# Swin block, linear attention and experts on one core: output projection, scores and values in side-by-side pieces of the array, gates spread by DMA, a 16-group body

## What is computed

```python
# layer 0: windows of 7x7, shifted by 3, 8 heads of 8 channels
y = _ln(x, ln1_w, ln1_b);  win = windows(roll(y, -3))          # 64 windows of 49 positions per image
attn = softmax(q @ k.T * 8**-0.5 + bias[rel_index] + attn_mask)
x = x + roll(windows_back((attn @ v) @ proj_w.T + proj_b), 3)
h = gelu(_ln(x, ln2_w, ln2_b) @ fc1_w.T + fc1_b)               # 256 hidden channels
x = x + _ln(h, ln3_w, ln3_b) @ fc2_w.T + fc2_b
# layer 1a: linear attention over a whole image, 16 heads of 4 channels, k and v normed per head
u = _ln_t(x);  kv = sum_n(k_n v_n.T) / 3136;  t = x + gelu((q @ kv + u) @ W_proj.T + b_proj) + u
# layer 1b: 8 experts per position, the 2 with the largest router logits
xn = _ln_t(t);  logits = xn @ Wr + br;  w, idx = top-2 softmax weights
e_i = gelu(norm(xn) * ln_g[i] + ln_b[i]) @ W1[i] + b1[i]) @ W2[i] + b2[i]
out = t + sum over the 2 chosen experts of w_i * e_i
```

## Time and profile before

| | before |
|---|---|
| median of 3 runs | 10356.69 us (10355.85 to 10370.08) |
| span of the profiled execution, first to last instruction | 10332.3 us |
| TensorE busy | 9863.4 us, 95% of the span |
| VectorE, ScalarE, GpSimd busy | 8358.3, 6196.1, 5266.7 us (81%, 60%, 51%) |
| mean granted TensorE clock | 0.978 |
| DMA | 6 GB/s |

### The profile page before, as it was taken

How to read it: one execution, slowest core, us unless ns; L and a number is a source line. 1 busy time by engine, 2 the same in 40 slices (tenths; PEclk the granted TensorE clock), 3 DMA queues, 4 the chain that set the end, 5 groups by cost and what they waited for, 6 DMA issues and landing times.

```text
span 10332.3 us, 296342 instructions
## 1 busy us (share of the span) xinstructions
PE 9863.4 (95%) x88046; PEld 8285.3 (80%) x88046; DVE 8358.3 (81%) x30953; ACT 6196.1 (60%) x10499; POOL 5266.7 (51%) x8196
## 2 busy tenths in 40 slices
PE   6799999999999999999999999999999999999998
PEld 4578888888888888888888888888888888888877
DVE  4478888888888888888888888888888888888873
ACT  1356666666666666666666666666666666666653
POOL 1245555555555555555555555555555555555542
PEclk9989999999999999999999999999999999999997
DMA  0000000000000000000000000000000000000000
GB/s 19 2 5 5 6 6 6 5 6 6 6 5 6 6 6 5 6 6 5 6 6 6 5 6 6 5 6 6 6 5 6 6 5 5 6 6 5 6 4 4
DMA packets 63043, 57.40 MB, mean 6 GB/s; under 512 B 11731, under 2 KB 62456, under 8 KB 62584
## 3 DMA queue, kind: packets, MB, share of 16 engines
q1 hardware_dynamic: 62840, 55.45, 1.8%
HBM read 29.57 MB, written 25.69 MB: 5 GB/s over the span
## 4 chain that ended last, share of the span: by engine, by line
PE 83%; DVE 11%; issue 4%; ACT 1%; POOL 1%; SPq 0%; DVEq 0%; DMA 0%; ACTq 0%; POOLq 0%
PE ps L704 22%; PE ps L695 12%; PE ps L512 7%; PE ps L488 7%; PE ps L440 5%; PE ps L551 4%; PE ps L576 3%; DVE hid L810 3%; PE ps L480 3%; PE ps L499 3%; PE ps L594 2%; DVE kvr L934 2%; PE ps L566 2%; PE ps L686 2%; PE ps L668 2%
## 5 line engine op out<-in xcount | busy, mean ns | idle before, releaser
L704 PEld LDWEIGHTS ps<-we,ht 128*98 128x98 f32 x32768 | 3149.3, 171 | 194.7 <-issue 90.3
L704 PE MATMUL ps<-we,ht 128*98 128x64 f32 x32768 | 3229.3, 253 | 39.2 <-DVE yg L1070 39.1
L1309 ACT ACTIVATE ht<-ps,be 128x392 f32<-128x392 f32 x4096 | 2283.7, 584 | 1279.9 <-PE ps L695 651.0
L1194 POOL TENSOR_TENSOR yacc<-yacc,yg 98x256 f32 (+1 forms) x1792 | 1385.1, 773 | 328.5 <-DVE yg L1070 265.6
L695 PE MATMUL ps<-xs,we_hi 128*128 128x392 f16 x4096 | 1386.1, 338 | 10.7 <-ACT ht L1309 10.3
L695 PE MATMUL ps<-xs,we_lo 128*128 128x392 f16 x4096 | 1378.0, 336 | 0.0
L1070 DVE TENSOR_TENSOR yg<-ps,gate 98x256 f32<-98x256 f32 x2048 | 860.8, 420 | 526.3 <-PE ps L704 473.3
L1125 POOL TENSOR_TENSOR sc<-sc,mx 98x392 f32<-98x392 f32 x1024 | 857.1, 847 | 528.7 <-DVE mx L854 524.9
L1135 POOL TENSOR_TENSOR x1b<-x,fc2bias 98x256 f32<-98x256 f32 x256 | 213.2, 833 | 1514.3 <-DVE x L888 1514.3
L488 PE MATMUL ps<-kexp,qbd 128*98 128x392 f32 x2048 | 895.8, 520 | 19.8 <-DVE sc L848 10.4
L233 POOL TENSOR_TENSOR kexp<-kt,cs 128x392 f32<-128x392 f32 x512 | 438.4, 856 | 855.0 <-ACT kt L1216 855.0
(11 more groups left out here) (175 smaller groups left out, 20077.8 us busy)
## 6 DMA issues: line engine op xcount, KB each, us to landing
xg<-in_x SPq DMA_DIRECT2D x256, 98.0 KB
out_y<-yo SPq DMA_DIRECT2D x256, 98.0 KB
bias<-in_rel SPq DMA_DIRECT2D x1, 1200.5 KB
bias<-in_w SPq DMA_DIRECT2D x2, 512.0 KB
tu_img<-in_amask SPq DMA_DIRECT2D x2, 300.1 KB
we<-in_w SPq DMA_DIRECT2D x1, 512.0 KB
cs<-in_cst SPq DMA_DIRECT2D x1, 163.0 KB
ht<-ht SPq DMA_DIRECT2D x2, 75.0 KB
```

What stands on the lines that cost most here:

```text
L704: last = pe.matmul(pY[0:TOK, C * t:C * (t + 1)], ht[:, 2 * (e % 2) + h, cols(t)], we2[:, 2 * e + h, :], start=(h == 0), stop=(h == 1))
L1194: pool.tensor_tensor(dst, acc, yg[:, e % 2:e % 2 + 1, :], ALU.add).then_inc(S["y_sum"], 1)
L1309: act.activation(ht[:, b % 4, :], pH[b % 2][:, 0:GTOK], ACT.Gelu, bias=be1[:, b:b + 1], scale=1.0 / WSCALE).then_inc(S["h_ready"], 1)
```

## The change

It rewrites most of the pipeline. Number of operations and shapes are for one group; the line numbers with L are those of the new file where they differ.

1. **Experts' output** (`expert_out`). The operands change places: `we2` (128x64) is the weight and the 392 positions of `ht` stream. Two experts stand side by side, one in the left 64 columns of the array and one in the right 64, and write different partitions of pY. Sixteen products of 392 columns take the place of 64 of 64 columns.
2. **Gates.** Since positions are now columns, a gate has to be spread over 64 partitions. The turned gates go to DRAM and come back with a copy per partition (`gates_away`, `gates_back`: one DMA of 12 KB out and four of 196 KB in). VectorE multiplies and adds the bias in one operation of 128x392 per pair of experts (`expert`), GpSimd adds three times, TensorE turns the sum back with a product against two stacked identities (`combine`), and `finish` on VectorE adds the residual. `gbias` and the eight small multiplications and additions go.
3. **Scores.** Eight products per pair of tiles, each with 32 rows and 64 columns of the array, 196 columns streaming: heads 0 to 3 and 4 to 7 in different rows and banks, the two windows in different columns. The zero blocks in `qbd` go (ScalarE copies the queries as they are), `kexp` has half the columns, and scores lie on 113 partitions (0 to 48 and 64 to 112).
4. **Values.** The values (98x32 for two heads) are the weight, 49 columns of the turned probabilities stream, four pieces side by side in the array. ScalarE copies the output, TensorE turns it back (four transposes of 128 columns, `back`), and VectorE needs one reciprocal and one multiplication.
5. **Third norm.** Its mean is subtracted in `wf2` beforehand, its scale is multiplied after `fc2` (`t`: four operations of 98x64). `ln3n` goes.
6. **Router.** xn is split into two f16 halves before it is turned over, logits come from f16 products with both halves. `max` and `max_index`, which give the eight largest values and their places, once a tile, take the place of the 13 steps.
7. **Buffers and body.** Ring buffers are addressed by constants in a body of 16 groups; statistics are kept twice; u and the residual stay in one buffer of 16 groups each; the second copy of the turned u and its copy back (`utk`, `utc`) go. The order of all steps is new: attention is now up to 4 groups ahead, experts 8 to 10 back.

```diff
-XBUF, YBUF = 4, 8
+BODY = 16
+XBUF, YBUF = 4, 2
...
             def score(a, t):
...
-                pe.matmul(pS[0:TOK, 0:HEADS * WA], qbd[:, t, :], kexp[:, t, :], start=True, stop=True)\
+                for t2 in range(2):
+                    t = 2 * pair + t2
+                    for half in range(2):
+                        for w in range(2):
+                            chans = slice(C * w + 32 * half, C * w + 32 * (half + 1))
+                            last = pe.matmul((pS, pO)[half][C * w:C * (w + 1), 4 * WA * t2:4 * WA * (t2 + 1)],
+                                             qs[chans, TOK * t + WA * w:TOK * t + WA * w + C], kexp[chans, t, :],
...
             def attend(a, t):
...
-                for h in range(HEADS // 2):
-                    last = pe.matmul(o[:, :, 2 * h:2 * h + 2, :], pt[:, t % 2, h, :],
-                                     vexp[:, 2 * t:2 * t + 2, 2 * h:2 * h + 2, :], start=True, stop=True)
+                for w in range(2):
+                    for hp in range(HEADS // 2):
+                        last = pe.matmul(pO[32 * hp:32 * (hp + 1), TOK * t + WA * w:TOK * t + WA * (w + 1)],
+                                         vexp[:, 2 * t + w, 2 * hp:2 * hp + 2, :].rearrange("p h d -> p (h d)"),
+                                         pt[:, t, hp, WA * w:WA * (w + 1)], start=True, stop=True)
...
+            def back(g):
+                bank_free(pe, "oT", g)
+                now(pe, "o_kept", g)
+                for t in range(GT):
+                    last = pe.transpose(pP[0:TOK, 128 * t:128 * (t + 1)], os_[:, cols(t)], ident)
...
-            def expert_out(d, e):
-                now(pe, "h_ready", d, 2 * e + 1)
-                now(pe, "yg_ready", d - (e == 0), (e - 1) % NE)
-                for t in range(GT):
-                    for h in range(2):
-                        last = pe.matmul(pY[0:TOK, C * t:C * (t + 1)], ht[:, 2 * (e % 2) + h, cols(t)], we2[:, 2 * e + h, :],
-                                         start=(h == 0), stop=(h == 1))
+            def expert_out(g, p):
+                bank_free(pe, f"out{p}", g)
+                now(pe, "h_ready", g, 0, 4 * p + 3)
+                for h in range(2):
+                    for e in range(2):
+                        b = 4 * p + 2 * e + h
+                        last = pe.matmul(pY[C * e:C * (e + 1), 0:GTOK], we2[:, b, :], ht[:, b % 8, :],
+                                         start=(h == 0), stop=(h == 1), skip_group_check=True)
+            def combine(g):
+                bank_free(pe, "comb", g)
+                now(pe, "y_sum", g)
+                for t in range(GT):
+                    last = pe.matmul(pY[0:TOK, C * t:C * (t + 1)], yg[:, 0, cols(t)], ii[:, :], start=True, stop=True)
...
+            def gates_back(g, half):
+                if half == 0:
+                    sp.wait_ge(gates_out, 16 * (g.n + 1))
+                now(sp, "yg_ready", g, -1, 2 * half + 1, alone="sp")
+                for e in range(2):
+                    sp.dma_start(gb[C * e:C * (e + 1), 2 * half:2 * half + 2, :],
+                                 gates_dram[g.j % 2].rearrange("(p e) q -> e p q", e=2)[e, 2 * half:2 * half + 2]
+                                 .partition_broadcast(C)).then_inc(gates_in[half], 16)
...
-            def ln3n(n, j):
-                normalize(n, "3", hn, lambda t: hid[:, t, :], "hn_ready")
+                for t in range(GT):
+                    last = dve.scalar_tensor_tensor(out=tt[:, g.j % 2, t, :], in0=pB[0:TOK, C * t:C * (t + 1)],
+                                                    scalar=rs["3"][:, g.j % 2, t:t + 1], in1=x1b[:, t, :],
+                                                    op0=ALU.mult, op1=ALU.add)
...
+                for t in range(GT):
+                    last = dve.max(best[:, t, :], lg[:, t, :])
+                for t in range(GT):
+                    dve.max_index(which[:, g.j % 2, t, :], best[:, t, :], lg[:, t, :])
```

More of the change, by code:

```diff
@@ L717, in _ @@
-            for b in range(2 * NE):
-                steps[f"in{b}"] = lambda d, j, b=b: expert_in(d, b)
-            for e in range(NE):
-                steps[f"out{e}"] = lambda d, j, e=e: expert_out(d, e)
-            for part in range(5):
-                steps[f"mix{part}"] = lambda i, j, part=part: mix(i, part)
-            images(pe, PLAN["pe"], steps)
+                steps[f"s{half}"] = lambda g, half=half: score(g, half)
+                steps[f"fc1{half}"] = lambda g, half=half: fc1(g, half)
@@ L726, in _ @@
+                steps[f"hT{half}"] = lambda g, half=half: hidden_T(g, half)
+            for b in range(BLOCKS):
+                steps[f"in{b}"] = lambda g, b=b: expert_in(g, b)
+            for p in range(PAIRS):
+                steps[f"out{p}"] = lambda g, p=p: expert_out(g, p)
+            for part in range(4):
+                steps[f"mixp{part}"] = lambda g, part=part: mix(g, part)
+            program(pe, PLAN["pe"], steps)
         @block.vector
-        def _(ve_):
-            dve = ve_
+        def _(dve):
+            dve.memset(gb[:, :, :], 0.0).then_inc(setup_dve, 1)
@@ L1316, in _ @@
+            steps = dict(zt=ln1n, qs=queries, kt=keys, os=keep_o, ot=oT, z2t=z2t, uts=keep_ut, sq=kv, sd=deviation, lpg=gp_,
+                         xh=split_high, xs=keep_xs, tanh=route, gtt=gates, exp=softmax_exp)
+            for half in range(2):
+                steps[f"ge{half}"] = lambda g, half=half: gelu(g, half)
+                steps[f"hnt{half}"] = lambda g, half=half: keep_hidden_T(g, half)
             for t in range(GT):
-                steps[f"pt{t}"] = lambda a, j, t=t: keep_pt(a, t)
```

1494 lines of the change are left out of this document (727 added, 767 removed).

## The result

| | before | after |
|---|---|---|
| median of 4 runs | 10362.67 us (10355.85 to 10370.08) | 8551.73 us (8542.04 to 8556.77) |
| ratio, 95% interval | | 0.8252 (0.8242 to 0.8262) |
| span of the profiled execution | 10332.3 us | 8551.3 us |
| mean granted TensorE clock | 0.978 | 0.984 |

The changed kernel takes 17.5% less time. The forecast of 8970 us had the sign and, within its range, the size, but lay 418 us too high; the number of rival (b), 8507 us, lay 45 us too low and was the nearer one.

What follows compares the result with a forecast made beforehand. TensorE was taken to bound the kernel: its terms sum to -5.7 us a group, 38.4 to 32.7, 32.8 with waits. 243 groups give 7970 us, plus 980 and 24: 8974, said as 8970; range 8450 to 9700.

Steps and rivals of the forecast that it cites:

- Experts' output: TensorE's expert products, two running side by side: 1.53 us a block, 6.1 us a group against 10.9, so -4.8.
- Scores: TensorE's score products, all four places at once: 0.9 us a block, 1.8 against 2.7 a group, -0.9, at worst +0.4.
- Values: TensorE's value products, four pieces at once: 0.45 + 0.25 us a block, 2.8 a group, +0.1, bounds -1.0 and +3.5.
- (b): Rival, everything as hoped: values at 0.2 us a block and waits gone, 31.0 us a group, 8507 us; 13%.
- allowance for waits: TensorE's own waits stay about the same; 0.1 us a group added, 32.7 to 32.8.
- Small steps: TensorE's other steps a group: logits -0.45 us, turned xn -0.1, turned probabilities +0.2, `back` +0.43, `combine` +0.69.
- The changes of form: Entering or leaving another form of TensorE's array costs 0.09 to 0.10 us each way, 22 times a group against six.
- all fit: The other engines' lists stay under 32.7 us a group: VectorE about 24, ScalarE 25.1, GpSimd about 18.
- Head and tail: Time outside the steady stretch, set-up included: left at 980 us of the 999 before.
- (a): Rival, waits between the lists from ScalarE, late gates or slower value records: 35.5 us a group, 9650 us; 22% with (d).
- (d): Rival, TensorE's clock falls to 1.2 GHz more often: some 2 us a group, near 9500 us; 22% with (a).
- (c): Rival, the array's pieces run one after another: +4.7 us, 43.1 us a group, 11550 us; 5%.

Runs made afterwards that it cites:

- part 4: The changed kernel with 32 groups in the loop body instead of 16: 8540.41 us; with the key product also moved behind the turning of z2: 8490.26 us.
- full-width kernel: The changed kernel with an output block's four products over the full width of the array, none beside another: 9280.28 us, 34.6 us a group.
- experiment 3: The changed kernel with unused work added: four VectorE reductions at its list's end 9195.27 us, or ahead of `u` 8607.06 us; eight ScalarE copies 8754.92 us.
- last kernel of part 4: The changed kernel with 32 groups in the loop body and the key product moved right ahead of the fourth output block: 8490.26 us, ratio 0.8213.

## Why the prediction was right, and where its numbers were off

- **The bound, and the sum's direction: right.** TensorE bounded the kernel and still does: 4.6 us more on its list made the group 2.8 us longer, while 2.2 us more on VectorE cost 0.2 us where it had room.
- **The sum fell short.** The most common group went from 37.8 to 31.0 us, 6.8 less, where the sum had 5.6 with its allowance for waits. Counted from each step's first record to the next step's, the missing 1.2 us are values 0.85, output, scores and hidden blocks 0.15 each, turned xn 0.1 and the allowance 0.1, less 0.25 that the logits took more. The mean fell by 0.2 less than that, 38.4 to 31.8, since the long groups of part 4 weigh more in it than those of the kernel before.
- **Experts' output: right.** Forecast 1.53 us a block with its changes of form, measured 1.47 and 0.1 ahead of it, 1.57. 6.3 us a group against 6.1. That the halves run at once, which had rested on the key product alone, shows in the starts of the records and in the full-width kernel.
- **Scores: right.** 0.9 forecast, 0.82 and 0.1 ahead measured. The row strips, for which no row spoke, run at once too.
- **Values: the mis-sized term.** I took 0.70 us a block out of a lower bound of 0.17, an upper of 1.3 and 0.25 for the forms. It is 0.31 and 0.1 ahead: four pieces' records start 7 ns apart, and the second, third and fourth four follow at 48, 23 and 28 ns. So 1.6 us a group, not 2.8, and 1.9 with 0.25 us behind one block in which TensorE waits for the gate. The end at 0.17 us a block was the right one for the records; I took a middle. By the Trainium skill's floor of 25 ns from start to start (TensorE: Matmul & The Clock Gate, Wait — 56ns, not 53.3ns?) I had found 0.4 us a block. Neither that floor nor the 62 ns holds between records of different pieces, which start 7 ns apart.
- **Waits: nearly the same in size, in other places.** In the kernel before 0.56 us stood behind one output block, where TensorE waited for VectorE's L1017; now 0.42 stand behind one, where it waits for ScalarE's `ht`. By the rows of the steady part TensorE waits for 1.4 us a group where it was 1.1. Taking them as unchanged was nearly right in size, though these are not the old ones.
- **Small steps: right within 0.3.** `back` 0.44 (forecast 0.43), `combine` 0.67 (0.69), turned probabilities 0.42 a block, +0.3 in all (+0.2); turned xn 0.17 in place of 0.36 (-0.2, forecast -0.1); logits 0.60 to the next start, where I had 0.35, most of the difference being a wait for VectorE's L891.
- **The changes of form: right.** 0.09 to 0.10 on either side: the step ahead of an output block lasts that much longer, and the block's last records stand 0.42 us ahead of the next step where they follow each other at 0.33. The Trainium skill's rule that a change of mode drains TensorE (TensorEngine Tiling (Array Packing), Key Properties) agrees with that price: in the full-width kernel the low half ahead of the output block takes 0.17 us, not 0.26.
- **VectorE, ScalarE, GpSimd: near as totals,** 25.8, 24.4 and 18.0 us a group against 24, 25 and 18. But "all fit" was argued from totals, and experiment 3 shows that this says little: 2.2 us cost 0.2 or 2.6 by their place.
- **Not foreseen: the jump back.** 6.7 us once in 16 groups, 0.4 a group. It was a price of the 16-group body that I had left out.
- **Head and tail: 815 us, not 980.** The thirteenth query product starts at 503 us where it started at 612, and the tail takes 312 where it took 387. I had moved both by 19 us together, though every step in them had got shorter.
- **The three errors add up.** 234 us of the period (243 groups at 31.8 instead of 32.8), 165 of head and tail and 24 between span and median are 423 us, against 422 between 8974 and the median.
- **The rivals.** (a) Waits between the lists exist, but only 0.35 us a group were added and not 2.7. In the kernel with the loaded end of VectorE's list they came with the clock, so (a) and (d) need not be two things. (b) The time lies 45 us from this rival's and the most common group has its 31.0 us, but not by its reasons alone: the waits are not gone, the mean group is 31.8, and 135 us less of head and tail than it had, with the 24 of the span, make up for most of that. (c) It is excluded by the starts of the records and by the full-width kernel.

## What to carry to other kernels

Where products are narrower than the array, put independent ones side by side: here two halves cost what one would alone, plus 0.1 us on each side for the change of form, and the order in which they were issued moved a block by no more than 0.02 us. But look at the waits and the clock behind it: the same step alone in the old kernel brought 0.85 of 4.4 us. Ask of every slack where it lies, since a total of 80% busy can hide a place with none, and look for TensorE's long waits: here those of 1.7 us at the gate and 3.3 us at the jump cost about double with the lower clock behind them, while a wait of 0.8 us once a group (last kernel of part 4) left the clock at 1.00.

## What the runs showed of the hardware that I had not expected

- Pieces of the array take instructions independently: a piece's product started 13 ns into the block although four records of another piece, 1.3 us of work, stood ahead of it.
- Four value records of 49 columns start 7 ns apart and the next four follow at 23 to 48 ns.
- An idle time of 1.8 us on TensorE was followed by 4.3 us at 0.6 of the clock, one of 3.6 us by 8 us at 0.69 and 0.50.
- The first 500 us of both kernels ran at half pace on TensorE, 0.84 us for a record that later takes 0.42, although it was busy for 82% and 78% of the head.
- A jump back over a body of 16 groups stops four engines for 2 to 3.6 us and costs 6.7 us with the clock; straight code ran at 31.7 us a group where the loop took 31.2, apart from groups at the low clock. The instruction queues carried 17.3 MB instead of 1.95.
